# A graph network's second attention: every fourth ramp on GpSimd, the pair's output copied by VectorE

## The reference, cut to what matters

```python
a_src = jnp.einsum('nhc,hc->nh', h, att_src)
a_dst = jnp.einsum('nhc,hc->nh', h, att_dst)
e = jax.nn.leaky_relu(a_src[src] + a_dst[dst], NEG_SLOPE)   # NEG_SLOPE = 0.2
m = jax.ops.segment_max(e, dst, num_segments=N)
ex = jnp.exp(e - m[dst])
s = jax.ops.segment_sum(ex, dst, num_segments=N)
alpha = ex / (s[dst] + 1e-16)
out = jax.ops.segment_sum(h[src] * alpha[:, :, None], dst, num_segments=N)
```

## Time and profile before

| | |
|---|---|
| median of 3 runs | 1726.23 us (1725.14 to 1726.70) |
| span of the profiled execution, its own time | 1723.2 us |
| that execution against the median | 3.0 us less |
| second attention, from its first ramp to the end of its last mask | 522 to 774 us |
| TensorE, VectorE, ScalarE, GpSimd busy over the span | 1572.0, 1300.9, 1177.9, 55.2 us |

### The profile page before, as it was taken

The page is one execution under the profiler, slowest core; times in us unless marked ns, Lnnn a source line. Parts: engine busy times, 40 slices in busy tenths (PEclk is TensorE's granted clock), DMA queues, the critical chain, the costliest instruction groups (busy, mean ns, idle before and its releaser), DMA issues. The chain is left out here.

```text
span 1723.2 us, 35023 instructions
## 1 busy us (share of the span) xinstructions
PE 1572.0 (91%) x14122; PEld 1429.3 (83%) x14122; DVE 1300.9 (75%) x2269; ACT 1177.9 (68%) x2181; POOL 55.2 (3%) x67
## 2 busy tenths in 40 slices
PE   7899799999995888798989999998799999999982
PEld 3788799999975777787978888888798888888882
DVE  6996999989468999995357777766733777777577
ACT  3455788888656999896457788873434777887434
POOL 0000000000000100000001000001100000000030
PEclk9899899999997999899999999999899999999995
DMA  4113222300006321112955333004067333200501
GB/s 180 55 53 101 83 70 76 122 31 2 1 1 176 120 91 61 61 32 86 245 151 150 91 89 85 16 2 134 1 158 205 94 78 78 64 2 1 123 5 59
DMA packets 76435, 139.33 MB, mean 81 GB/s; under 512 B 16849, under 2 KB 50353, under 8 KB 74992
## 3 DMA queue, kind: packets, MB, share of 16 engines
q1 hardware_dynamic: 76272, 137.06, 28.2%
HBM read 96.22 MB, written 29.45 MB: 73 GB/s over the span
## 5 line engine op out<-in xcount | busy, mean ns | idle before, releaser
L2125 DVE CUSTOM_DVE_ANT_0 probs_att<-banks,logs_or_y 125x1250 f32<-125x1250 f32 x160 | 233.6, 1460 | 124.9 <-PE banks L2019 123.5
L1028 PE MATMUL banks<-ident,probs_gat 125*125 125x125 f32 x1600 | 214.1, 283 | 46.7 <-ACT probs_gat L1132 46.1
L2081 ACT COPY probs_t_att<-banks 125x375 f32<-125x375 f32 (+1 forms) x480 | 205.0, 532 | 72.1 <-PE banks L2029 72.1
L2073 ACT ACTIVATE probs_att<-probs_att,neg_max_att 125x1250 f32<-125x1250 f32 x160 | 218.4, 1365 | 48.5 <-DVE neg_max_att L2125 48.5
L1028 PEld LDWEIGHTS banks<-ident,probs_gat 125*125 125x125 f32 x1600 | 194.7, 195 | 57.3 <-ACT probs_gat L1132 57.1
L1132 ACT ACTIVATE probs_gat<-probs_gat,neg_max_gat 125x1250 f32<-125x1250 f32 x160 | 214.7, 1342 | 34.3 <-DVE neg_max_gat L1301 33.8
L1301 DVE CUSTOM_DVE_ANT_0 probs_gat<-probs_gat,log_counts 125x1250 f32<-125x1250 f32 x160 | 236.8, 1480 | 0.1
L2040 PE MATMUL banks<-probs_t_att,v_rows 125*64 125x125 f32 x3200 | 189.5, 272 | 0.9 <-ACT feature_cols L2088 0.9
L2029 PE MATMUL banks<-ident,probs_att 125*125 125x125 f32 x1600 | 189.3, 273 | 0.0
L1039 PE MATMUL banks<-h,probs_t_gat 125*125 125x128 f32 x1600 | 188.9, 274 | 0.0
L2040 PEld LDWEIGHTS banks<-probs_t_att,v_rows 125*64 125x64 f32 x3200 | 170.6, 136 | 19.5 <-ACT probs_t_att L2081 17.7
(11 more groups left out here) (258 smaller groups left out, 2892.9 us busy)
## 6 DMA issues: line engine op xcount, KB each, us to landing
a_pair<-a_src_rows SPq DMA_DIRECT2D x46, 625.0 KB, 4.8
q_first<-q_rows SPq DMA_DIRECT2D x12, 1000.0 KB, 11.2
logs_or_y<-log_rows SPq DMA_DIRECT2D x20, 546.9 KB
q_rows<-q_out_qkv SPq DMA_DIRECT2D x40, 250.0 KB, 4.6
q_att<-q_rows SPq DMA_DIRECT2D x8, 1000.0 KB, 10.8
w_rows<-in_L_gnn_W_dram SPq DMA_DIRECT2D x12, 512.0 KB, 13.7
log_counts<-counts_fr SPq DMA_DIRECT2D x50, 122.1 KB
k_halves<-k_low_qkv SPq DMA_DIRECT2D x20, 250.0 KB, 3.9
```

The costliest lines, as they stand in the source:

```text
L1028: block_t = pe.transpose(turned(u)[:, i // 2, (i % 2) * P:(i % 2 + 1) * P], probs[:, u % PROBS, i * P:(i + 1) * P], k.ident[0:P, 0:P])
L2073: act.activation(probs[:, u % SLOTS], probs[:, u % SLOTS], ACT.Exp, scale=-1.0, bias=neg_max[:, column(u)], accum_out=sums[:, column(u)]). ...
L2081: act.copy(probs_t[:, u % TURNED, lo:hi].rearrange("p c n -> p (c n)"), turned(u, j)).then_inc(piece_saved, 1)
L2125: dve.tensor_tensor_reduce(probs[:, u % SLOTS], scores, logs[:, t % KEPT], -1.0, -FLOOR, ALU.add, ALU.min, neg_max[:, column(u)]).then_inc ...
```

## The change

- For the units 83, 87, ..., 159 of the second layer (`pooled(u)`, 20 of 80) VectorE no longer makes the ramp. GpSimd makes it in two operations, max(0.2 a, knee) times 4, plus 0.2 a, in a buffer of its own with two places, `pool_ramps`. It may start on its ramp i as soon as the mask of its ramp i-2 is done (8 units back). The mask of such a unit reads that buffer and writes into `probs`; it waits for `pool_ramped` and for `probs_turned`, which the ramp waited for until now.
- `knee` is a new column operation of 125x80 on VectorE ahead of the stage.
- The copy of a pair's product moves from ScalarE to VectorE, one step later in n, between the sums and the mask of an even step; the last two come after the loop.
- GpSimd's four subtractions for the next stage come after its ramps 3, 5, 7 and 9.
- SyncE's loads of a row pair also wait for GpSimd's ramps.
- The program is built with a DMA scratch of 4096 bytes, which leaves more of SBUF for buffers.

```diff
+    EVERY = 4
+    RISE = (1.0 - NEG_SLOPE) / NEG_SLOPE
...
+        pool_ramps, knee = sb("pool_ramps", [P, 2, N]), sb("knee", [P, T, H])
...
+        def pooled(u):
+            return u >= PER and (u - PER) % EVERY == EVERY - 1
...
             for part in range(2, 2 * H):
-                sp.wait_ge(ramp_done, first_unit(part - 1))
+                sp.wait_ge(ramp_done, own_before(first_unit(part - 1)))
+                sp.wait_ge(pool_ramped, pooled_before(first_unit(part - 1)))
                 load_pair(1, part % H)
...
-                if n >= PER + 5 and n % 2 == 1 and n - 5 < UNITS:
-                    copy_out(n - 5)
...
+            def ramp(u):
+                _, head, t = place(u)
+                i = pooled_before(u)
+                part = head + H * (t >= A)
+                pool.wait_ge(a_loaded[head % 2], 32 * ((H - 1) // 2 + (part + 1) // 2))
+                if i == 0:
+                    pool.wait_ge(spread_saved, len(spans))
+                    pool.wait_ge(gap_done, 2)
+                if i >= 2:
+                    pool.wait_ge(masked, u - 2 * EVERY + 1)
+                low_row = gat.pair[0:P, head % 2, 1]
+                pool.tensor_scalar(pool_ramps[:, i % 2], low_row, knee[:, t, head:head + 1], RISE, ALU.max, ALU.mult
+                                   ).then_inc(pool_bent, 1)
+                pool.wait_ge(pool_bent, i + 1)
+                pool.tensor_tensor(pool_ramps[:, i % 2], pool_ramps[:, i % 2], low_row, ALU.add).then_inc(pool_ramped, 1)
+
+            for u in range(PER, UNITS):
+                if pooled(u):
+                    ramp(u)
+                    i = pooled_before(u)
+                    if i % 2 == 1 and 3 <= i < 3 + 2 * NEXT:
+                        lower_next((i - 3) // 2)
...
-                dve.wait_ge(ramp_done, u + 1)
-                dve.tensor_tensor_reduce(probs[:, u % PROBS], probs[:, u % PROBS], k.log_counts[:, t],
+                ramped = probs[:, u % PROBS]
+                if pooled(u):
+                    ramped = pool_ramps[:, pooled_before(u) % 2]
+                    dve.wait_ge(pool_ramped, pooled_before(u) + 1)
+                    dve.wait_ge(probs_turned, u - PROBS + 1)
+                else:
+                    dve.wait_ge(ramp_done, own_before(u) + 1)
+                dve.tensor_tensor_reduce(probs[:, u % PROBS], ramped, k.log_counts[:, t],
...
+            def copy_out(u):
+                pair = pairs_before(u)
+                dve.wait_ge(summed, PER + pair + 1)
+                if pair >= 2:
+                    dve.wait_ge(turned_back, pair - 1)
+                dve.tensor_copy(out_cols[:, pair % 2], cols_bank(pair)).then_inc(out_copied, 1)
...
-                    if live(layer, n + 2):
+                    if live(layer, n + 2) and not pooled(n + 2):
                         ramp(n + 2)
...
                         safe_pair(n - 2)
+                        if n >= PER + 6:
+                            copy_out(n - 6)
...
+            dve.tensor_scalar(knee[:], a_all[:, :, 1], -NEG_SLOPE, None, ALU.mult).then_inc(gap_done, 1)
             attend(1)
+            for u in range(UNITS - 4, UNITS, 2):
+                copy_out(u)
...
-    nc = bacc.Bacc("TRN2", target_bir_lowering=False, num_devices=1)
+    nc = bacc.Bacc("TRN2", target_bir_lowering=False, num_devices=1, dynamic_dma_scratch_size=4096)
```

More of the change, by code:

```diff
@@ L903, in stage_gat @@
         out_copied, turned_back = k.sem("out_copied_gat"), k.sem("turned_back_gat")
+        pool_ramps, knee = sb("pool_ramps", [P, 2, N]), sb("knee", [P, T, H])
+        pool_bent, pool_ramped = k.sem("pool_bent_gat"), k.sem("pool_ramped_gat")
         a_loaded = [k.sem(f"a_loaded{i}_gat") for i in range(2)]
@@ L932, in pairs_before, with pooled_before, own_before @@
             return (u - PER) // 2
+        def pooled(u):
+            return u >= PER and (u - PER) % EVERY == EVERY - 1
+        def pooled_before(u):
+            return max(0, u - PER) // EVERY
+        def own_before(u):
+            return u - pooled_before(u)
         def column(u):
@@ L1150, in save_out @@
                 act.activation(result, out_bank(u), ACT.Copy, scale=inverse[:, column(u)]).then_inc(final_done, 1)
[L1152 to L1157, removed]
             def save_pair(u):
@@ L1274, in _, with lower_next @@
         def _(pool):
-            for c in range(NEXT):
+            def lower_next(c):
                 pool.wait_ge(next_high_done, c + 1)
                 pool.tensor_tensor(next_w[2][:, c], next_w[0][:, c], next_w[1][:, c].bitcast(F32), ALU.subtract).then_inc(next_low_done, 1)
+            def ramp(u):
[19 more added lines that the diff above has]
+                        lower_next((i - 3) // 2)
         @block.vector
```

## The result

The changed kernel takes 1816.22 us (median of 4 runs, 1815.28 to 1818.35) against 1726.47 us for the kernel before: a ratio of 1.0534, with a 95% interval of 1.0516 to 1.0552. It is 90 us slower. The forecast was slower by 52 us, with a range up to 1818 us; the ratio times the 1726.23 us of then is 1818.4, 0.4 us above its upper end. The sign was right and the size short by 38 us.

A forecast was written before the change was run, and what follows sets the result against it. VectorE was taken to bound the second attention (243 of 252 us). -28.6 + 7.6 + 82 - 5.3 - 2.9 - 1.2 + 0.1 = +51.7 us, giving 1778 us beside 1726.2; range 1750 to 1818.

The forecast's parts named there:

- What bounds the stage: Second attention: VectorE's work, 243 of 252 us, sets the pace at 5.76 us a pair; ScalarE would be next at 5.57.
- Ramps removed and copies added: Second attention, VectorE: 20 ramps of 1.43 us go, -28.6 us; copies from PSUM at 0.20 us come, +7.6 us.
- The hold of the addition: GpSimd's second operation for a ramp, two inputs of 1250 columns, holds VectorE up for 2.6 us.
- The hold of the first operation: GpSimd's first operation for a ramp, one tensor input, holds VectorE up for 1.5 us.
- whole durations: GpSimd's operations block VectorE for their full length: 2.75 + 3.56 = 6.3 us a ramp, 126 us in place of 82.
- What swallows some of it: Second attention: row-pair wait absorbs 5.3 us, VectorE's waits for TensorE go, 2.9, and ScalarE's end follows sooner, 1.2.
- The sum: Whole change: +51.7 us, with 82 us of it from GpSimd's holds on VectorE, 4.1 us for each of 20 ramps.
- The rivals: Other outcomes for the second attention: faster 0.06, short holds (1739 or 1748 us) 0.08, longer 0.10, no change 0.02.
- the longer ones: Second attention: whole durations block, 1822 us, or TensorE's clock falls, 44 us again; chance 0.10.
- The faster one: Second-attention rival: GpSimd takes only what VectorE leaves, if both holds together stay under 1.03 us; 1719 or 1708 us; chance 0.06.
- What VectorE's operations wait for: Second attention: masks and ramps beside GpSimd's operations lengthen, one by 1.5 and one by 2.6 us for each GpSimd ramp.

The follow-up runs named there:

- the light operation: Kernel before, with GpSimd making one mult and add for each of 20 units, max and second addition left out, copy on ScalarE: 1721.32 us, ratio 0.9972.

## Why the prediction was right in sign and short in size

- *What bounds the stage*: right. VectorE, and its holds, set the pace; ScalarE waited 92.9 us for masks.
- *Ramps removed and copies added*: right. The copy's queue time was forecast at 0.20 us, 7.6 in all; in the trace it is 0.20 (from the copy's start at 638.58 to the mask's at 638.78), and the kernel with the copy alone is 7.8 us slower. That the two totals agree to 0.2 us is luck, since the interval is 4 to 11.
- *The hold of the addition*: right. Taken 2.6, bounds 2.26 to 3.56; 2.3 from end to end, 2.2 in the rows.
- *The hold of the first operation*: **this is the term that failed.** Taken 1.5, bounds 1.2 to 2.75; it is 3.3 from end to end, 3.6 in the first block and 3.5 in the later ones. All three figures came from the earlier trace rows, where the 250-column operations are mult and add. The change has max and mult. The rows were near in engine, form and operands, but the arithmetic was another, and on GpSimd that is a factor of 3.4 (4.51 against 1.32 us). Even "whole durations" wasn't an upper bound. With the first operation left out, the forecast's own sum gives 1778 - 20 x 1.5 = 1748, and the addition alone measures 1.0146 x 1726.2 = 1751, so the rest of it stood to some 3 us.
- *What swallows some of it*: half right. The wait of 5.7 us for the row pair is gone. The 2.9 us of waits for TensorE weren't; they grew to 21.0, but 19.4 of those lie inside holds, so counting none of them was right in effect.
- *The sum*: 20 x (3.3 + 2.3) = 112 us in place of 82 adds 30 to the forecast's 52. The prices from end to end already have in them what was absorbed, so that the other 8 us are near the 9.4 it had subtracted follows from how they are made and shows nothing by itself. An estimate from the rows does: 20 x 5.7 us of holds - 28.6 + 7.6 = 93, and the stage grew by 90, so some 3 us were absorbed.
- *The rivals*: the longer ones name 1822, nearer to the ratio's 1818.4 than the forecast is, and yet neither is what happened. Whole durations of 2.75 and 3.56 us were wrong for both operations, one too short and one too long, and came out near by luck. The clock did fall, to a mean of 0.79 in the stage, but VectorE lost at most the 1.6 us that stand outside the holds. The faster one decides at holds under 1.03 us together, which is the ramp's 1.43 less the 0.4 of the copies. No run tested that figure: the light operation (0.97 in the block shown) is faster, but its copies stand on ScalarE, so its limit is 1.43; the addition alone (2.3) is over both and is slower. Of the 7.6 us that the rival promised 4.8 came, and nothing for 3 us taken off VectorE in another way.
- *What VectorE's operations wait for*: the forecast thought of the ramps and masks. The small addition, which has one SBUF tensor, took 38 us of the blocking (40 at 1113 ns in place of some 160).

## What to carry to other kernels

Before an elementwise operation is moved from VectorE to GpSimd, compare not the two durations but the time that GpSimd's operation holds VectorE up with the time that it saves there, and take it from a row of the same arithmetic: here max and mult on 1250 columns cost VectorE 3.3 us, an addition of two tensors 2.3, mult and add 0.8, for a ramp of 1.43. A bound worked out from rows with another operation code is not a bound. Where an engine bounds a stage by a few per cent only, relief of it can be worth less than the sum of its rows: here up to 3 us saved were given back in a later stage, where TensorE's clock fell.

## What the runs showed of the hardware

- On GpSimd max takes 3.44 us alone for 125x1250 float32 and 4.51 with a mult, where mult and add take 1.32.
- A tensor_scalar or an SBUF-to-SBUF copy on VectorE waits for GpSimd as an operation with two SBUF inputs does, even with two columns (it takes 2.4 us beside an addition, 4.3 beside max and mult); reciprocal (0.155), reduce (1.446), a copy from PSUM and an addition with a PSUM operand (0.409) don't. The Trainium skill (SBUF — State Buffer, the section on two separate sides) names two SBUF inputs and the two-port modes as what locks; the rows agree as far as they go, and the two-column case shows that the width doesn't matter.
- For a VectorE operation with two SBUF inputs the hold is shorter than GpSimd's operation: 3.6 of 4.4 us after its turn, 0.97 of 1.32. A tensor_scalar of two columns beside max and mult ended only with it (4.26 us, from 0.3 us into its 4.51).
- GpSimd doesn't always get its turn at the end of the running VectorE operation. Beside the earlier trace rows it did after the ramp; in the changed kernel 15 of the 20 first operations, some 6.99 us long against 4.51 alone, waited through the ramp and nearly the whole mask, which was issued after them and kept its 1.45 us. What decides this wasn't tried.
